# Token stage of an attention and ternary-FFN block: normed rows split in fp16 halves, stored, and read back by transposing transfers instead of being transposed on TensorE

## What is computed

```python
xn = layer_norm(x)                                   # x: 8 x 1024 x 512, float32
qkv = xn @ W_qkv.T                                   # 1536 columns
attention over 16 heads of 32, then @ W_o.T
h = bitlinear(xn, w_fc)                              # norm, 8-bit round trip, ternary weights: 2048 columns
h = gelu(h);  f = bitlinear(h, w_proj)               # back to 512 columns
out = x + attention_output + f
```

## Time and profile before

| what | value |
| --- | --- |
| median of three runs | 3477.92 us |
| the profiled execution, its own time | 3480.74 us |
| its span (first to last instruction) | 3478.8 us |
| mean granted TensorE clock | 0.978 of full speed |
| busy share: PE, DVE, ACT, POOL | 96%, 70%, 57%, 57% |
| first product of the token stage | 102.17 us |
| last product of the token stage | 1539.83 us |

### The profile page before, as it was taken

One profiled execution on the slowest core, in us unless ns is written; L12 is line 12 of the kernel. 1 busy time (PEld: TensorE's weight loads), 2 busy tenths in 40 slices (PEclk: granted clock), 3 DMA queues, 4 the chain that ended last, 5 costly groups with the idle time before them and its releaser, 6 DMA issues.

```text
span 3478.8 us, 56956 instructions
## 1 busy us (share of the span) xinstructions
PE 3328.9 (96%) x17648; PEld 1369.2 (39%) x17648; DVE 2421.4 (70%) x3450; ACT 1993.5 (57%) x2949; POOL 1966.7 (57%) x690
## 2 busy tenths in 40 slices
PE   3899999999999999989999999999999999999798
PEld 2444444444444444432333333333333333333233
DVE  6676666666666666668777777777777777777134
ACT  3444444444444444425777777777777777777511
POOL 0322222323323233215999898989989899899600
PEclk7899999999999999987999999999999999999999
DMA  4122222222222222233333333433433332331277
GB/s 169 73 69 90 84 93 80 87 79 88 88 88 85 83 83 84 81 85 60 81 72 68 78 72 64 84 70 66 84 70 66 77 77 66 76 76 44 71 275 259
DMA packets 376034, 308.49 MB, mean 89 GB/s; under 512 B 300672, under 2 KB 317056, under 8 KB 365440
## 3 DMA queue, kind: packets, MB, share of 16 engines
q1 hardware_dynamic: 375744, 304.69, 32.6%
HBM read 96.99 MB, written 139.46 MB: 68 GB/s over the span
## 4 chain that ended last, share of the span: by engine, by line
PE 45%; DMA 3%; issue 2%; DVE 2%; POOL 1%; ACT 1%; SPq 0%; DVEq 0%; POOLq 0%; ACTq 0%
PE outputs L1061 14%; PE es_for_maxima_and_scores L1070 13%; PE es_for_maxima_and_scores L1049 12%; PE misc L1094 5%; DVE half_maxima L985 2%; DMA k_stackT<-attention_scratch 2%; DMA out<-q_stackT 1%; POOL probs_sum L906 1%; ACT probs L938 1%; PE es_for_maxima_and_scores L1127 1%; DVE q_stackT L1027 0%; ACT k_stackT L944 0%; DMA q_stackT<-stack_scratch 0%; PE misc L1078 0%; SPq L891 0%
## 5 line engine op out<-in xcount | busy, mean ns | idle before, releaser
L985 DVE TENSOR_REDUCE half_maxima<-es_for_maxima_and_scores 128x1 f32<-128x512 f32 x2048 | 1275.4, 681 | 368.4 <-PE es_for_maxima_and_scores L1070 368.2
L938 ACT ACTIVATE probs<-es_for_maxima_and_scores,scalars 128x512 f32<-128x512 f32 x2048 | 1256.8, 690 | 420.4 <-PE es_for_maxima_and_scores L1049 420.1
L906 POOL TENSOR_TENSOR probs_sum<-probs_sum,probs 128x2048 f32<-128x2048 f32 x256 | 1163.4, 4545 | 16.9
L1070 PE MATMUL es_for_maxima_and_scores<-k_stackT,q_stackT 96*128 96x512 f16 x2048 | 802.2, 393 | 21.7 <-DMA q_stackT<-stack_scratch 11.2
L1049 PE MATMUL es_for_maxima_and_scores<-q_stackT,k_stackT 98*128 98x512 f16 x2048 | 781.9, 384 | 27.5 <-issue 18.4
L1061 PE MATMUL outputs<-probs,v_rows 128*32 128x512 f32 x4096 | 544.9, 604 | 1.2 <-ACT probs L938 0.8
L402 POOL TENSOR_TENSOR gelu_sum<-gelu_sum,gelu_out 128x1024 f32<-128x1024 f32 x96 | 254.9, 2655 | 451.5 <-ACT gelu_out L577 451.5
L1070 PEld LDWEIGHTS es_for_maxima_and_scores<-k_stackT,q_stackT 96*128 96x128 f16 x2048 | 200.0, 98 | 622.5 <-DVE half_maxima L985 467.6
L906 POOL TENSOR_TENSOR probs_sum<-probs 128x2048 f32<-128x2048 f32 x64 | 291.4, 4553 | 210.4 <-ACT probs L938 210.4
L640 PE MATMUL psA<-x_hi,ternary_fcT 128*128 128x512 f16 x1024 | 389.9, 381 | 1.5 <-DVE x_lo L448 1.4
L1049 PEld LDWEIGHTS es_for_maxima_and_scores<-q_stackT,k_stackT 98*128 98x128 f16 x2048 | 295.2, 145 | 241.3 <-ACT probs L938 46.9
(11 more groups left out here) (126 smaller groups left out, 3172.0 us busy)
## 6 DMA issues: line engine op xcount, KB each, us to landing
stack_scratch<-hi_hi_lo_hi_rows SPq DMA_DIRECT2D x32, 1536.0 KB, 5.1
stack_scratch<-hi_hi_lo_hi_rows SPq DMA_DIRECT2D x32, 576.0 KB, 5.9
v_scratch<-v_rows_out SPq DMA_DIRECT2D x32, 576.0 KB, 6.9
x_rows<-in_L_attn_x SPq DMA_DIRECT2D x16, 1024.0 KB, 4.8
x_plus_ffn_scratch<-x_rows SPq DMA_DIRECT2D x16, 1024.0 KB, 3.9
v_rows<-v_scratch SPq DMA_DIRECT2D x32, 512.0 KB, 4.0
inverse_denominators<-denominators_scratch SPq DMA_DIRECT2D x256, 64.0 KB, 2.0
attention_scratch<-out_normed SPq DMA_DIRECT2D x64, 256.0 KB, 2.1
```

What stands on the lines that cost most here:

```text
L906: nc.gpsimd.tensor_tensor(acc[:, hf], pr[:, 0] if j == 1 else acc[:, hf], pr[:, j], ALU.add).then_inc(added, 1)
L938: nc.scalar.activation(pr[:, w % 8, h, :], psS[:, bank(HG * w + h), :], ACT.Exp, scale=keep["scal"]["escale"]).then_inc(exp_done, 1)
L985: nc.vector.tensor_reduce(mx[:, slot(n, 2), h, t, kh:kh + 1], psX[:, bank(r), :], axis=AX.X, op=ALU.max).then_inc(max_done, 1)
L1070: nc.tensor.matmul(psX[:, bank(r), :], qT[0:STACK, slot(n, 4), h, t * P:(t + 1) * P], kT[0:STACK, slot(n, 4), h, kh * BANK:(kh + 1) * BANK ...
```

## The change

x2 stays as rows. ACT now copies the whole of x2 (128 x 2048) to fp16 rows `xhr`; DVE writes the rest, `xlr`, as fp16 rows over the first half of x2. SP stores each half (512 KB) into a DRAM scratch `xt_dram`, waits for both, and reads them back by eight transposing transfers (each 512 rows by 128 columns, 128 KB) into xh and xl. PE transposes nothing in this stage, and waits at the start of a step for all eight transfers.

The work for t+1 moves inside step t: on DVE `stats` from unit 5 to unit 2, `normed` from the second product to unit 4, `low` to unit 5; on ACT `high` to unit 5, between the evacuations of u = 7 and u = 8; on POOL `norm` from the end of the sums to after the sum of j = 3. On SP the waits and stores of the halves stand after the store of i = 1, the wait for both halves in DRAM stands ahead of the store of i = 2, and the eight transfers behind it. SP's steps are written out one by one, without a loop.

To make room for `xhr`, `vrow` has one buffer instead of two, with one semaphore; in an odd step the first evacuation of every i waits for the store of the i before it.

```diff
-        vrow = sb("v_rows_out", [P, 2, E3])
+        vrow = sb("v_rows_out", [P, E3])
+        xhr = sb("x_hi_rows", [P, 4, D], F16)
+        xlr = x2[:].rearrange("p i d -> p (i d)").bitcast(F16)[:, 0:4 * D].rearrange("p (i d) -> p i d", i=4)
...
+            def store_halves(t, s):
+                sp.wait_ge(xh_ready, lin(t, 1, 1))
+                sp.dma_start(xt_dram[s][0].rearrange("i p d -> p i d"), xhr[:]).then_inc(xt_stored, 16)
+                sp.wait_ge(xl_ready, lin(t, 1, 1))
+                sp.dma_start(xt_dram[s][1].rearrange("i p d -> p i d"), xlr).then_inc(xt_stored, 16)
+
+            def load_halves(t, s):
+                for half, dst in enumerate((xh, xl)):
+                    rows = xt_dram[s][half].rearrange("i p d -> (i p) d")
+                    for c in range(CD):
+                        sp.dma_start_transpose(dst[:, s, c, :], rows[:, c * P:(c + 1) * P]).then_inc(xt_loaded[s], 16)
+
+            store_halves(0, 0)
+            sp.wait_ge(xt_stored, 32)
+            load_halves(0, 0)
+
             def body(t, s, has_next):
...
                 for i in range(4):
+                    if i == 2 and has_next:
+                        sp.wait_ge(xt_stored, lin(shift(t, 1), 32, 32))
                     sp.wait_ge(b_out, lin(t, 12, 3 * i + 3))
...
-                        sp.dma_start(v_v[batch(t)][V_ROW:P, i, :], vrow[V_ROW:P, i % 2, :]).then_inc(v_stored[i % 2], 16)
+                        sp.dma_start(v_v[batch(t)][V_ROW:P, i, :], vrow[V_ROW:P, :]).then_inc(v_stored, 16)
+                    if i == 1 and has_next:
+                        store_halves(shift(t, 1), 1 - s)
+                    if i == 2 and has_next:
+                        load_halves(shift(t, 1), 1 - s)
...
+                    if j == 3 and has_next:
+                        norm(shift(t, 1), 1 - s)
...
-                wait(dve, t_full, lin(t, 4))
+                wait(dve, xh_ready, lin(t, 1))
+                wait(dve, xt_stored, lin(t, 32))
...
+            def low(t):
+                dve.wait_ge(xh_ready, lin(t, 1, 1))
+                nc.vector.tensor_tensor(xlr, x2[:], xhr[:], ALU.subtract).then_inc(xl_ready, 1)
...
+                    if j == 2 and has_next:
+                        stats(shift(t, 1), 1 - s)
+                    if j == 4 and has_next:
+                        normed(shift(t, 1), 1 - s)
                     if j == 5 and has_next:
-                        stats(shift(t, 1), 1 - s)
+                        low(shift(t, 1))
...
+            def high(t):
+                act.wait_ge(x2_ready, lin(t, 1, 1))
+                wait(act, xt_stored, lin(t, 32))
+                nc.scalar.copy(xhr[:], x2[:]).then_inc(xh_ready, 1)
...
-                        wait(act, v_stored[i % 2], turn(t, 32) + 16 * (i // 2))
+                        wait(act, v_stored, turn(t, 64) + 16 * i)
...
                     for u in qkv_of[j][:1]:
                         evacuate(t, s, u)
+                    if j == 5 and has_next:
+                        high(shift(t, 1))
...
-            def transposes(t, s, chunks, first=False):
...
-                pe.wait_ge(xl_ready, lin(t, 4, 4))
+                pe.wait_ge(xt_loaded[s], turn(t, 128) + 128)
...
-                    elif i < 3 and has_next:
-                        transposes(shift(t, 1), 1 - s, (2 * i - 2, 2 * i - 1))
```

More of the change, by code:

```diff
@@ L359, in body @@
                     if s == 1:
-                        sp.dma_start(v_v[batch(t)][V_ROW:P, i, :], vrow[V_ROW:P, i % 2, :]).then_inc(v_stored[i % 2], 16)
+                        sp.dma_start(v_v[batch(t)][V_ROW:P, i, :], vrow[V_ROW:P, :]).then_inc(v_stored, 16)
[3 more added lines that the diff above has]
+                        load_halves(shift(t, 1), 1 - s)
                 sp.wait_ge(y_ready, lin(t, 4, 4))
                 sp.dma_start(yx_v[at(t)], xs[:, s]).then_inc(y_stored[s], 16)
-            steps(sp, body)
+            for t in range(STEPS):
+                body(t, t % 2, t < STEPS - 1)
             for k in range(2):
@@ L367, in _ @@
                 sp.wait_ge(stack_stored[k], 16 * STEPS * 2)
-                sp.wait_ge(v_stored[k], 16 * STEPS)
+            sp.wait_ge(v_stored, 16 * 4 * STEPS // 2)
         @block.gpsimd
@@ L519, in body @@
                                                    ALU.mult, ALU.add).then_inc(y_ready, 1)
[L520 to L523, removed]
             stats(0, 0)
             normed(0, 0)
-            low(0, 0, range(CD))
+            low(0)
             steps(dve, body)
@@ L563, in evacuate @@
                 else:
-                    nc.scalar.activation(vrow[:, i % 2, cols], psB[:, u % 2, :], ACT.Copy,
+                    nc.scalar.activation(vrow[:, cols], psB[:, u % 2, :], ACT.Copy,
                                          scale=rc[:, s, i:i + 1]).then_inc(b_hi, 1)
@@ L586, in body @@
                         evacuate(t, s, u)
-                if has_next:
-                    high(shift(t, 1), 1 - s, range(CD))
-            high(0, 0, range(CD))
+            high(0)
             steps(act, body)
@@ L594, in _ @@
         def _(pe):
-            def transposes(t, s, chunks, first=False):
[L597 to L602, removed]
-                    elif c == 1 and not first:
-                        pe.wait_ge(b_out, lin(t, 12))
-                    for i in range(4):
-                        last = nc.tensor.transpose(psB[:, c % 2, i * P:(i + 1) * P],
-                                                   x2[:, i, c * P:(c + 1) * P], keep["id32"][:])
-                    last.then_inc(t_full, 1)
             def project_qkv(t, s, u):
@@ L612, in project_qkv @@
                 wait(pe, b_out, lin(t, 12, u - 1))
+                if u == 0:
+                    wait(pe, st_out, lin(t, 1))
                 cols = slice(third * BANK, (third + 1) * BANK)
@@ L657, in body @@
                         hidden_sums(t)
-                    elif i < 3 and has_next:
-                        transposes(shift(t, 1), 1 - s, (2 * i - 2, 2 * i - 1))
-            transposes(0, 0, range(CD), first=True)
             steps(pe, body)
@@ L1147, in build @@
     v_dram = nc.dram_tensor("v_scratch", (B, TT, E3), F32).ap()
+    xt_dram = nc.dram_tensor("x_halves_scratch", (2, 2, 4, P, D), F16).ap()
     yx_dram = nc.dram_tensor("x_plus_ffn_scratch", (B * L, D), F32).ap()
```

11 lines of the change are left out of this document (5 added, 6 removed).

## The result

The change makes the kernel slower. The kernel after takes 3577.06 us (median of four runs, 3574.82 to 3585.1) against 3477.10 before: a ratio of 1.029, with a 95% interval of 1.028 to 1.030. The forecast was 3573, range 3520 to 3635. All times compared here are of fast executions: one of the kernel of experiment 3 took 5861.79 us, with a granted clock of 0.621 on the mean, and its ratio goes without it.

A forecast was written before the change was run, and what follows sets the result against it. TensorE was taken to bound the token stage. Transposes - 26.4, first step + 12, even steps + 4, odd steps + 101, step 15 + 5 make + 95.6 on 3480.74: 3576.3, less 2.8 for the median, 3573; range 3520 to 3635.

The forecast's parts named there:

- step 15, up to the attention stage's first product: Last odd step, without halves or statistics: waits for the single v buffer cost 5 us, 3 to 7.
- The transposes, 0.88 us a group: Two groups of TensorE transposes vanish from each of 15 steps, all on the path: 26.4 us less.
- The first step: Nothing covers its preparation, stores and eight transfers: first product near 114, 12 us late, 9 to 20.
- Even steps: Work moved inside the step just fits on DVE: 0.5 us a step, 0 to 2, 4 us in eight steps.
- The waits in an odd step: TensorE waits through the single v buffer: 0.55, 0.7, 2.2, 0.6 and 7.5 us, in all 11.6, in seven steps.
- The clock: Behind the 7.5 us wait in odd steps TensorE's granted clock halves, costing 2.8 us, bounds 0 and 2.8.
- The halves ahead of the third store: On SP in odd steps the third v store queues behind the halves; TensorE waits 7.5 us ahead of u = 11.
- The transfers inside a step: Eight transfers, pipelined 10 to 14 us, are hidden by the second product: 34 us available in even steps, over 40 in odd.
- (1): Stores land within the slack, third v store of odd steps under 3.3 us; kernel gets faster, 3463.5; 7 in 100.
- (2): Transposing transfers are slow, from 4.3 us each in even steps: 3640 to near 3870; 5 in 100.
- (4): Odd steps cost only 9 us, for instance halves land in 1.5 us and the clock stays up: 3526; 16 in 100.
- (3): DVE bounds even steps too, through meetings with POOL additions: 28 us instead of 4, 3597; 12 in 100.

The follow-up runs named there:

- experiment 3: Kernel before with vrow in one buffer instead of two, nothing else changed: 3550.24 us, ratio 1.020; run once more, 3549.27 us.
- experiment 8: Kernel after with two v buffers, four transfers, waits chunk by chunk, and in unit 5 the low part of u = 7 ahead of h_lo: 3464.26 us.
- experiment 6: Kernel after with two v buffers and xh, xl side by side, so four transfers of 256 KB replace eight: 3472.04 us, ratio 0.998 to kernel before.
- experiment 4: Kernel after with 20 unused products ahead of u = 11 in the seven odd steps with a next: 3593.69 us, ratio 1.033 to kernel before.
- experiment 5: Kernel after with 36 unused products ahead of u = 11 in the seven odd steps with a next: 3565.80 us, ratio 1.025 to kernel before.
- experiment 1: Kernel after with the halves' stores and the wait for them moved on SP behind the store of i = 2: 3558.04 us, ratio 1.023 to kernel before.
- experiment 2: Kernel after with vrow in two buffers again and xhr placed in the next step's xh: 3474.61 us, ratio 0.9992 to kernel before.

## Why the prediction was right

The reading that TensorE bounds the stage, so that both what is removed and what makes it wait count one for one, held: the changes of its steps add up to the change of the stage. Against before, each a mean from the starts of the steps in the two traces, steps 2 to 14 for the even ones:

| term | forecast us | measured us |
| --- | --- | --- |
| first product of the stage | + 12 | + 11.95 |
| an even step (transposes off, small waits on) | - 1.26 | - 1.31 |
| an odd step with a next one | + 12.6 | + 12.53 |
| step 15, up to the attention stage's first product | + 5 | + 4.5 |

Step 0 is 2.55 us shorter and not 1.26. The forecast had left out that it begins at half the clock: that lasted 5.7 us in the kernel before (102.17 to 107.8) and 3.7 here (114.12 to 117.8; the window 116 to 118 has 0.54), about 1 us of work less. Together 11.95 - 2.55 - 7 x 1.31 + 7 x 12.53 + 4.5 = 92.4, the 92.5 of the stage.

Point by point:

- *The transposes, 0.88 us a group.* Right: 89.78 - 2 x 0.88 = 88.02, and the last experiment has steps of 88.03.
- *The first step.* The sum was right by two errors that cancel. The second store landed in 2.9 us, not 3.5, the normed rows came 1.3 us earlier than in the profile of before, but each issue cost 1.29 us, not the value between 0.7 and 1.3. The trace of before had shown 256 KB only; experiment 6 shows that between these two sizes the queue makes next to no difference. That the value came out at 12 was luck.
- *Even steps.* Right: 88.2 to 88.6 behind the first.
- *The waits in an odd step.* Forecast 0.55, 0.7, 2.2, 0.6 and 7.5, together 11.6; measured 0.42, 0.21, 1.87, 1.38 and 7.06, together 10.9. The wait ahead of u = 11 has two errors that cancel: the halves landed in 2.95 us and not 3.5, and the third v store took 7.8, not 6.9. The wait ahead of u = 9 was mis-sized: the normed rows took 4.02 us beside a POOL addition, not 1.91. The profile of before had the sign of it, an addition of 3.01 in place of 1.21 beside POOL, and I had not applied it to this operation.
- *What a wait costs beside its idle time.* Left out. A product takes 0.38 us from start to end and the next one starts after 0.216, so each wait costs 0.16 more than its idle time. Five make 0.8. For the step: 88.03 + 10.94 + 0.8 + clock = 101.97 leaves 2.2 for the clock, forecast 2.8; in the other odd steps whose waits are all on record it is 1.6 to 2.7.
- *The clock.* The cost was right within 0.6 us a step, its condition was not. "7.5 is well over 4.6" took the one fall in the trace of before for a threshold; it fell behind waits of 2.7 us (experiment 4) and 3.3 us (experiment 3) as well, and behind waits of 2.0 us: four times in experiment 3, and in step 1 of the kernel after (a wait of 2.05 us, the products again from 250.12, the clock 0.74 in the window from 250 and 0.50 in the next). Other waits of 1.7 to 2.0 us left it at full, one of 2.04 among them (step 1 of experiment 5). What decides between them is open.
- *The halves ahead of the third store.* The place was right, the share wasn't. The forecast put all 7.5 us under this heading. Experiment 1 takes the halves out of the way and 4.6 us remain: the order on SP is worth 19 us in the whole kernel, and the single buffer alone, in the kernel before, 71 (experiment 3). With the moved work and the order of experiment 1 it is worth 83 (3558.04 against the 3474.61 of experiment 2): there TensorE waits ahead of u = 6 and 9 too, 0.21 and 1.37 us, which it doesn't in experiment 3. The single buffer is the cause that matters; with two buffers the order costs nothing (experiment 2).
- *The transfers inside a step.* Hidden, in even steps too: no step but the first begins with a wait for them. The Trainium skill, "VectorE: DVE Perf Modes", section "The three transpose paths", gives 1309 ns for a block of 128 x 128 by DMA. As a price for each block of a larger transfer this is not borne out: a transfer of four blocks costs the queue 1.29 us in all and lands 2.8 to 3.4 us after its issue (medians); no run has a transfer of one block. "Advanced Engine Details and Errata" of the Trainium skill, section "X-Bar Transpose (TRN2)", has transposes as fast as plain transfers. This isn't shown either, though the prediction took the trace to side with it: 128 KB in 1.29 us is 102 GB/s, the 256 KB of experiment 6 in 1.36 are 193, and at the start of the stage 1 MB comes back in 12.0 us by eight transfers (102.13 to 114.12) and in 7.7 by four (102.68 to 110.38), where a plain transfer of 1 MB lands in 3.9.
- *Rivals.* (1) was out: no v store landed in under 6.9 us, and its data, 576 KB, isn't small beside the 512 KB of a half. (2) was out with the transfers hidden. (4) was out: the halves took 2.95 us to land, not 1.5, and the clock fell in each of the seven odd steps. (3), VectorE as the bound in even steps, was there in small: 0.39 us ahead of u = 9 in four of the seven even steps from 2 to 14 and 0.31 in one, and experiment 8 took such waits away.

## What to carry to other kernels

When a change needs room, look at what gave the room: here halving a staging buffer cost about 71 us, while the transposes that the room was for were worth 26. Before a double buffer is given up, set the landing time of its store (6.9 us from its issue) against the time from that issue until its first writer comes again (1293.38 - 1290.50 = 2.9 us), and look for a buffer that is dead at that time; the next step's input buffer was, and cost nothing. A wait of the engine that bounds the stage costs more than its idle time: 0.16 us in the pipeline, and behind some waits of 2 us and more, and all of 4.3 us and more in the token stage of these runs, a fall of the clock worth about 2 us.

## What the runs showed of the hardware

- TensorE's granted clock halved behind idle stretches of 2.0 to 7.1 us, at times only after the products had begun again (experiment 3: new start at 635.91, the window from 636 has 0.76 and the next 0.50), and it cost 1.6 to 2.7 us a time in the kernel after. Two stretches of 3.3 us and most of those of 2.0 left it at full. Filling the gap with useless products gave 11 us back.
- A transposing transfer costs the SP queue 1.29 us at 128 KB and 1.36 at 256 KB with nothing ahead of it (start of the stage). Behind a stack and a v store of 576 KB each, four of 128 KB took 9.0 us (kernel after, step 13).
- A store of 512 KB landed in 2.95 us alone; a v store of 576 KB, 0.4 us behind a stack store of the same size, in 7.1 with nothing behind it and in 7.8 with the transposing transfers behind it.
- Four VectorE operations of 0.54 us each (float32, one tensor operand from SBUF, 512 columns) took 4.02 us together beside a GpSimd addition of 2.36 us, where 1.91 is the time alone.
- The same unchanged attention stage took 1926 to 1938 us in ten profiled executions; a difference of a few us in one span can't be put down to the stage before it.
